# Diagonal blocks of a Gram matrix as high times half of high plus high times low, with their transposes taken up in the head weights

## The reference

```python
mn = (m - mu) * jax.lax.rsqrt(var + EPS) * gamma + beta
q = (mn @ Wq).reshape(N, L, H, C)
k = (mn @ Wk).reshape(N, L, H, C)
...
att = jnp.einsum('slhc,tlhc->sth', q, k) * scale
att = jax.nn.softmax(att, axis=1)
o = jnp.einsum('sth,tlhc->slhc', att, v) * g
```

## Time and profile before

| | us |
|---|---|
| median of 3 runs | 2096.09 |
| lowest and highest | 2093.72, 2096.11 |
| profiled execution, its own time | 2093.88 |
| its span, first to last instruction | 2092.2 |
| PE busy | 1981.6 (95%) |
| DVE busy | 1237.8 (59%) |
| ACT busy | 674.5 (32%) |
| POOL busy | 440.5 (21%) |

### The profile page before, as it was taken

One profiled execution on the slowest core, in us unless ns is written; L12 is line 12 of the kernel. 1 busy time (PEld: TensorE's weight loads), 2 busy tenths in 40 slices (PEclk: granted clock), 3 DMA queues, 4 the chain that ended last, 5 costly groups with the idle time before them and its releaser, 6 DMA issues.

```text
span 2092.2 us, 27450 instructions
## 1 busy us (share of the span) xinstructions
PE 1981.6 (95%) x9540; PEld 1640.6 (78%) x9540; DVE 1237.8 (59%) x2227; ACT 674.5 (32%) x1091; POOL 440.5 (21%) x565
## 2 busy tenths in 40 slices
PE   7999999999999999999999999999999999438898
PEld 6888888888888888788888878888888788327797
DVE  4656565665656556756565565656654478756543
ACT  4422222222222226322222222222222266424454
POOL 3302020211202014302020220202012155422342
PEclk9999999999999999999999999999999999769999
DMA  4232433334343333143333424333334479310110
GB/s 141 91 101 83 156 114 121 101 120 156 94 141 111 122 119 122 61 166 116 121 111 121 149 72 161 110 121 111 111 131 171 176 278 310 124 31 21 41 42 31
DMA packets 88114, 250.14 MB, mean 120 GB/s; under 512 B 11968, under 2 KB 32448, under 8 KB 88000
## 3 DMA queue, kind: packets, MB, share of 16 engines
q1 hardware_dynamic: 84928, 240.27, 34.4%
q0 software_dynamic: 3072, 8.44, 1.3%
HBM read 194.05 MB, written 54.62 MB: 119 GB/s over the span
## 4 chain that ended last, share of the span: by engine, by line
PE 90%; DVE 5%; issue 2%; ACT 1%; DMA 1%; POOL 1%; SPq 0%; DVEq 0%; ACTq 0%; POOLq 0%
PE bank L662 34%; PE bank L677 34%; PE bank L809 4%; PE bank L1563 4%; PE bank L1583 3%; PE bank L712 3%; PE bank L1151 2%; PE bank L634 2%; PE bank L647 1%; PE bank L608 1%; PE bank L618 1%; DVE top_passed L1232 1%; DVE top_counts L1235 0%; DVE top_pivots L1229 0%; DMA prelu<-in_tok_prelu_a 0%
## 5 line engine op out<-in xcount | busy, mean ns | idle before, releaser
L677 PE MATMUL bank<-x_hi,kt 128*128 128x512 f32 x2048 | 724.2, 395 | 1.5 <-DVE work L518 1.4
L518 DVE SCALAR_TENSOR_TENSOR work<-bank,d_col,gate 128x512 f32<-128x512 f32 x512 | 383.9, 750 | 553.7 <-PE bank L677 544.4
L397 ACT ACTIVATE p_hi<-work 128x512 fp32r<-128x512 f32 x512 | 324.1, 633 | 1065.7 <-PE bank L662 1020.6
L677 PEld LDWEIGHTS bank<-x_hi,kt 128*128 128x128 f32 x2048 | 384.4, 188 | 90.7 <-DVE work L518 2.7
L662 PE MATMUL bank<-p_hi,v_hi 128*128 128x512 f32 x1024 | 407.0, 397 | 0.3 <-ACT yT L359 0.2
L662 PE MATMUL bank<-p_hi,v_lo 128*128 128x512 f32 x1024 | 404.1, 395 | 0.0
L662 PE MATMUL bank<-p_lo,v_hi 128*128 128x512 f32 x1024 | 403.4, 394 | 0.0
L677 PE MATMUL bank<-x_lo,kt 128*128 128x512 f32 x1024 | 400.9, 392 | 0.0
L506 DVE TENSOR_TENSOR p_lo<-work,p_hi 128x512 fp32r<-128x512 f32 x512 | 367.7, 718 | 29.3 <-ACT p_hi L397 29.2
L567 POOL TENSOR_SCALAR spread<-mv 128x4 f32<-128x4 f32 x16 | 5.0, 310 | 1125.6 <-DVE mv L450 1125.6
L662 PEld LDWEIGHTS bank<-p_hi,v_hi 128*128 128x128 f32 x1024 | 192.2, 188 | 50.6 <-DVE p_lo L506 5.3
(11 more groups left out here) (227 smaller groups left out, 2281.3 us busy)
## 6 DMA issues: line engine op xcount, KB each, us to landing
gate<-in_gateT SPq DMA_DIRECT2D x256, 512.0 KB, 3.6
work<-in_xT SPq DMA_DIRECT2D x32, 512.0 KB, 4.9
scratch_rows<-rows SPq DMA_DIRECT2D x16, 518.0 KB, 3.8
scratch_h<-work SPq DMA_DIRECT2D x16, 512.0 KB, 3.0
scratch_mn<-mn_sb SPq DMA_DIRECT2D x16, 512.0 KB, 6.8
scratch_mT_hi<-mT_hi SPq DMA_DIRECT2D x16, 512.0 KB, 2.7
scratch_mT_lo<-mT_lo SPq DMA_DIRECT2D x16, 512.0 KB, 4.0
gate<-scratch_mn SPq DMA_DIRECT2D x16, 512.0 KB, 4.4
```

What stands on the lines that cost most here:

```text
L397: nc.scalar.activation(p_hi[:, i % 2, :], p32[:, i % RP, :], ACT.Copy).then_inc(hi_done, 1)
L518: nc.vector.scalar_tensor_tensor(p32[:, i % RP, :], S[i % 2][:, :], d_col[:, i:i + 1], gate[:, g % RG, j, :], ALU.add, ALU.mult).then_inc( ...
L677: mm = pe.matmul(S[i % 2][:, :], w, x, start=n == 1, stop=n == 3 * KD)
```

## The change

The diagonal blocks G(0,0) and G(1,1) are symmetric. With H the high part and L the low part, the block is H^T H + H^T L + L^T H. The changed kernel sums B = H^T (H/2) + H^T L alone, so that B + B^T is the block. It leaves the product low by high out for the diagonal blocks, and in `head_weights` B enters twice: once with Wk first and Wq as the factor, once with Wq first and Wk as the factor. G(0,1) is summed as before.

ACT therefore makes four tiles for each chunk in the place of one instruction: the high parts of entry 0 (`g_own`) and entry 1 (`g_other`), then half of the high part of entry 0 (`g_other`) and of entry 1 (`g_own`), so that `g_other[:, h, :, tile]` is H(0)/2 beside H(1), one moving operand of 512 columns. DVE makes the low part in two instructions, one for each entry. SP's load and PE's first product wait for all four copies.

```diff
@@ -226,8 +226,8 @@
         g32 = gate[:, :, :, :].rearrange("p (h b) g t -> p h b (g t)", h=2)
-        g_hi, g_lo = (W["kt"][:, :, :, :].rearrange("p i k t -> p (i k t)")[:, i * 4 * TPC * D:(i + 1) * 4 * TPC * D]
-                      .rearrange("p (h b n) -> p h b n", h=2, b=2) for i in range(2))
+        g_other, g_own, g_lo = (W["kt"][:, :, :, :].rearrange("p i k t -> p (i k t)")[:, i * 4 * TPC * D:(i + 1) * 4 * TPC * D]
+                      .rearrange("p (h b n) -> p h b n", h=2, b=2) for i in range(3))
         S, Y, TR = pr.banks[0:2], pr.banks[2:4], pr.banks[4:8]
@@ -338,6 +338,7 @@
                 past(sp, g_lo_ok, c - 1)
+                past(sp, g_hi_ok, c * 4 - 4)
                 for s in range(2):
@@ -410,7 +411,8 @@
                 past(act, g_done, c - 1)
-                nc.scalar.activation(g_hi[:, h], g32[:, h], ACT.Copy).then_inc(g_hi_ok, 1)
+                for tile, s, half in ((g_own, 0, 1.0), (g_other, 1, 1.0), (g_other, 0, 0.5), (g_own, 1, 0.5)):
+                    nc.scalar.activation(tile[:, h, s], g32[:, h, s], ACT.Copy, scale=half).then_inc(g_hi_ok, 1)
                 if early(c, 1):
@@ -539,8 +541,10 @@
             def gram(c, h):
-                dve.wait_ge(g_hi_ok, c + 1)
-                nc.vector.tensor_tensor(g_lo[:, h], g32[:, h], g_hi[:, h].bitcast(F32), ALU.subtract).then_inc(g_lo_ok, 1)
+                for s, tile in enumerate((g_own, g_other)):
+                    dve.wait_ge(g_hi_ok, c * 4 + s + 1)
+                    low = nc.vector.tensor_tensor(g_lo[:, h, s], g32[:, h, s], tile[:, h, s].bitcast(F32), ALU.subtract)
+                low.then_inc(g_lo_ok, 1)
                 if early(c, 1):
@@ -698,19 +702,22 @@
                 pe.wait_ge(g_lo_ok, c + 1)
+                pe.wait_ge(g_hi_ok, c * 4 + 4)
                 for j in range(TPC):
-                    for i in range(4):
-                        s, m = i // 2, i % 2
-                        if early(c, 1) and j == 0 and i == 2:
+                    tile = slice(j * D, (j + 1) * D)
+                    for m in range(KD):
+                        cols = slice(j * D + m * P, j * D + (m + 1) * P)
+                        first = early(c, 1) and j == 0
+                        high, low = g_own[:, h, 0, cols], g_lo[:, h, 0, cols]
+                        pe.matmul(G[m][:, 0:2 * D], high, g_other[:, h, :, tile], start=first, stop=False, skip_group_check=True)
+                        pe.matmul(G[m][:, 0:2 * D], high, g_lo[:, h, :, tile], start=False, stop=False, skip_group_check=True)
+                        pe.matmul(G[m][:, D:2 * D], low, g_other[:, h, 1, tile], start=False, stop=False, skip_group_check=True)
+                    for m in range(KD):
+                        if early(c, 1) and j == 0 and m == 0:
                             pe.wait_ge(y_evac, END * 2)
-                        cols = slice(j * D + m * P, j * D + (m + 1) * P)
-                        tile = slice(j * D, (j + 1) * D)
-                        out = G[i][:, 0:2 * D] if s == 0 else G[i][:, 0:D]
-                        for n, (w, x) in enumerate(split_products(
-                                g_hi[:, h, s, cols], g_lo[:, h, s, cols],
-                                g_hi[:, h, s:2, tile], g_lo[:, h, s:2, tile])):
-                            mm = pe.matmul(out, w, x, start=early(c, 1) and j == 0 and n == 0,
-                                           stop=False, skip_group_check=True)
+                        high = g_other[:, h, 1, j * D + m * P:j * D + (m + 1) * P]
+                        pe.matmul(G[2 + m][:, 0:D], high, g_own[:, h, 1, tile], start=first, stop=False, skip_group_check=True)
+                        mm = pe.matmul(G[2 + m][:, 0:D], high, g_lo[:, h, 1, tile], start=False, stop=False, skip_group_check=True)
                     if early(c, 1) and j == 0:
@@ -827,22 +834,23 @@
-        for i, (g0, c0, w) in enumerate(((0, 0, wk), (0, D, wq), (0, D, wk), (2, 0, wk))):
-            if i == 3:
-                pe.wait_ge(prod_ok, 1)
+        for i, (g0, c0, w) in enumerate(((0, 0, wk), (0, 0, wq), (0, D, wq), (0, D, wk), (2, 0, wk), (2, 0, wq))):
+            if i >= 3:
+                pe.wait_ge(prod_ok, i - 2)
             for m in range(KD):
                 for k in range(KD):
                     mm = pe.matmul(TP[i % 3][:, m, :], grams[:, g0 + k, c0 + m * P:c0 + (m + 1) * P], w[:, k, :],
                                    start=m == 0 and k == 0, stop=k == KD - 1, skip_group_check=True)
             mm.then_inc(tp, 1)
         pe.wait_ge(made, 2 + P // head)
-        for i in range(4):
+        for i, of in enumerate((0, 0, 1, 2, 3, 3)):
             pe.wait_ge(prod_ok, i + 1)
             for j in range(KD):
                 for m in range(KD):
-                    at = 4 * i + 2 * j
+                    at = 4 * of + 2 * j
                     mm = pe.matmul(colp[:, at:at + 2], prod[:, i, m, j * P:(j + 1) * P], heads_in["ones"][:, :],
-                                   start=i == 0 and j == 0 and m == 0, stop=m == KD - 1, skip_group_check=True)
+                                   start=i == 0 and j == 0 and m == 0, stop=m == KD - 1 and i not in (0, 4),
+                                   skip_group_check=True)
         mm.then_inc(col_ok, 1)
@@ -854,7 +862,7 @@
         dve.wait_ge(ld, 16 * 7)
-        for i, w in enumerate((wq, wk, wq, wq)):
+        for i, w in enumerate((wq, wk, wk, wq, wq, wk)):
             dve.wait_ge(tp, i + 1)
@@ -947,7 +955,7 @@
-            sp.wait_ge(pr.sem("hw_tp"), 4)
+            sp.wait_ge(pr.sem("hw_tp"), 6)
             sp.dma_start(mlp_raw["w1"], ins["ffn_w1"].rearrange("(k p) n -> p k n", p=P)).then_inc(raw_ld, 16)
@@ -1662,7 +1670,7 @@
                     [(x, [P, KD, width]) for x in ("v", "g", "k", "q", "o_wr")] + [("o", [P, KD, width + 2])] +
-                    [("prod", [P, 4, KD, width]), ("same_head", [P, P]), ("ones", [P, 2]), ("cols", [P, 16]),
+                    [("prod", [P, 6, KD, width]), ("same_head", [P, P]), ("ones", [P, 2]), ("cols", [P, 16]),
                      ("att", [P, 2, 2, 2]), ("top", [P, 2, 2]), ("shifted", [P, 2, 2, 2]), ("expd", [P, 2, 2, 2]),
                      ("total", [P, 2, 2]), ("inv", [P, 2, 2])])}
                 start_mix(pr, W2, heads_in, M, scratch, pr.last_mnT)
```

## The result

Seven executions of each kernel give a median of 2095.17 us before and 2088.77 us after. The ratio is 0.9968, with a 95% interval from 0.9956 to 0.9979: 6.7 us faster (4.4 to 9.2). The forecast was 2087.5 us, with 8.6 us to be gained. The direction and the order of size are right; about 2 us of the gain are missing, and they can be found.

What follows compares the result with a forecast made beforehand. PE, busy for 95% of the span, was taken as the bound. Terms of -13.06, -0.74 and +5.20 us summed to -8.6 us: 2085.3 us from the profiled 2093.88, forecast as 2087.5 given the runs' median; range 2083.8 to 2091.8 us.

Steps and rivals of the forecast that it cites:

- Term 1: Gram stage, chunks 1 to 7: fewer long products on PE, 6.58 us a chunk against 8.445, -13.06 us.
- term 2: Gram stage, chunk 0: DVE's chain decides when PE begins chunk 1, 1584.7 us instead of 1585.44, -0.74 us.
- Term 3: Head weights: groups and sums over rows go from 32 to 48 instructions each on PE, +5.20 us.
- The clock rival: After the head weights: low clock may start within the longer sums, -1.8 to +3.6 us; chance 0.12 for the upper half.
- The other rivals: DVE held by POOL (0.08), weights late (0.05), chunk loads as bound (0.04), no gain where claimed (0.05).
- POOL did hold DVE up: Gram stage, subtractions for chunks 2 and 3: each loses 2.1 us to POOL, 3.1 us in all; chance 0.08.
- the row with 4.41 us: Chunk 3 before the change: DVE's subtraction took 4.41 us where 2.3 is usual, beside four POOL additions.
- The chunk loads: Gram stage: loads become the bound if a landing exceeds 8.5 us; about 2100.3 us at 12.7 us landings, chance 0.04.
- The head weights were not late: Ahead of the head weights' use at L816: weights ready at 1635.4 us, PE waits 3.8 us; chance 0.05.

Runs made afterwards that it cites:

- gram_only: Changed kernel's new Gram stage with the old head weights (four groups, diagonal transposes left out), against the kernel before: ratio 0.9946, 11.3 us faster.
- low_first: Changed kernel with DVE's low parts of chunk 1 ahead of rectifying and moments, chunk 2 ahead of normalisation: ratio to the kernel before 0.9955, 9.4 us faster.
- head_only: Old Gram stage with the new head weights (six groups, diagonal blocks counted twice), against the kernel before: ratio 1.0032, 6.7 us slower.
- gram_only_2: Second execution of the new Gram stage with the old head weights, profiled: stage 60.02 us, with a low stretch.
- before_again: The unchanged kernel profiled once more: stage 72.24 us, no low stretch.
- after_again: The changed kernel run again, against the kernel before: ratio 0.9962, 8.0 us faster; stage 60.01 us.
- all_three: Changed kernel with low parts moved up, diagonal groups added by DVE before the sums, and keep_y ahead of ACT's fourth copy: ratio to the kernel before 0.9945.
- low_first_2: Second profiled execution of the changed kernel with DVE's low parts of chunks 1 and 2 moved up: stage 56.18 us, no low stretch.
- after: First profile of the changed kernel: stage 60.02 us with a low stretch; the kernel's median 2088.77 us.
- before: First profile of the unchanged kernel: stage 72.24 us, no low stretch; the kernel's median 2095.17 us.

## Why the prediction was right, and what it lacked

**Term 1 (chunks 1 to 7) and term 2 (chunk 0)** came to 13.8 us in the sum and to 13.77 us in gram_only with the clock up. PE started 0.25 us earlier after the last product of the tokenizer (forecast 0.4) and chunk 1 0.67 us earlier (forecast 0.74). PE's wait ahead of chunk 1 was forecast as 2.2 us and measured as 2.0 us, and its releaser was DVE's low part. Moving that part up (low_first) gave those 2 us back, which shows that the chain through rectifying and moments decided there.

**Term 3 (head weights)**: forecast 5.20 us. The work itself was priced rightly: 3.45 us for the groups and 1.79 us for the sums at the full clock. But to the end of the 48 products it cost 6.2 to 6.3 us in all three profiles, because more work of PE lay in the low stretch, in the sums or behind them. The prediction had put this clock change at nothing; it is the second size that was off, by 1.0 us.

**The step that was mis-sized most** is the price of PE's wait ahead of chunk 1. The prediction took it as 2.2 us, with the clock at the full level behind it. It costs its own length and, in most profiles, another 1.5 us. This is the term by which the stage's gain was 12.2 us instead of 13.8. With the 6.2 us of the head weights the sum is -13.8 + 1.5 + 6.2 = -6.1 us. From the tokenizer's last product to the end of the 48 products, the three profiles of the changed kernel take 100.0 us and the two of before 106.0 us: 6.0 us less. The measured 6.7 us agree with that within their interval. The interval of the ratio would also hold -8.6 us; the stages don't.

**The clock rival** was right in its mechanism and its bounds, but at only one of two places: I looked for a fall in the sums and for a longer low stretch behind them (found, 1.0 us in the changed kernel and 2.7 us in head_only) and not behind the new wait. The Trainium skill (TensorE: Matmul & The Clock Gate, "What's actually happening") says that the monitor runs freely and does not start with the kernel. The trace agrees as far as gram_only and gram_only_2 can show it, with 58.47 and 60.02 us for one and the same kernel, wait and stage. That this is the reason for the difference is not shown.

**The other rivals** did not occur. POOL did hold DVE up: the two subtractions for chunk 3 took together 3.18 us in place of 2.35,

```profile
1588.70 2.35 DVE L546 TENSOR_TENSOR kt<-gate,kt 128x1024 fp32r<-128x1024 f32 x2
1596.14 3.18 DVE L546 TENSOR_TENSOR kt<-gate,kt 128x1024 fp32r<-128x1024 f32 x2 [5.09 <-ACT kt L415]
```

but the loss was 0.8 us, not 4.2, and PE waited for nothing there. That is near to one POOL operation of 0.7 us and so nearer to the lock rule of the Trainium skill (SBUF — State Buffer, "SBUF: two separate sides") than to the row with 4.41 us. Nor does that row stand for the kernel before. In before_again POOL began its four additions as far ahead of DVE, and this time POOL lost the time (4.89 us instead of 2.84) and DVE none:

```profile
1596.27 4.89 POOL L580 TENSOR_TENSOR work<-work,attn_bo 128x256 f32<-128x256 f32 x4
1596.84 2.33 DVE L543 TENSOR_TENSOR kt<-gate,kt 128x2048 fp32r<-128x2048 f32 x1 [6.03 <-ACT kt L413]
```

Which of the two gives way differed between two executions of one kernel; why is not known. The price of this rival was also counted too high: if chunk 2 comes 2.3 us late, PE needs chunk 3 only at 1600.2 us, and even with both losses it is there by then, so the sum is 2.3 us and not 3.1. The chunk loads never held ACT back: it idled for PE alone ahead of its copies of chunks 2 to 7. The head weights were not late; PE had no wait ahead of L816 at 1635.01 us.

**Left open**: what decides in a given execution whether the clock falls behind a wait of 2.0 us, and the rest of the kernel. From the end of the 48 products to the end of the span, ten of the fourteen profiles take 412.9 to 413.4 us. The others take 410.3 (after_again), 410.6 (gram_only_2), 414.2 (low_first) and 416.0 us (all_three), and it is not known why. low_first_2 has 413.4, so the same kernel differs there by 0.8 us, and after_again and after by 2.8 us. A single execution can't show a gain of 6 us to better than that.

## What to carry to other kernels

Where PE is the bound, a sum over its products by the pace of long chains came within 0.1 us here, and a short stall within 0.2 us, by following the one engine that comes late. But a stall of PE had two prices, its length and, in six of eight profiles, 1.5 us for the low clock behind it. So the cheapest gain behind such a change may be to reorder the engine that is late, here 3.8 us for moving DVE's low parts of two chunks up. Many tiny products (two columns each) were a place for a low clock as well, and adding their inputs first on an engine with room took 1.7 to 2.6 us off. And where a low stretch stands, measure to the end of the work that it can reach: a part that ran at the full clock may only have pushed the loss into the next.

## What the runs showed of the hardware that was not expected

- A PE wait of 2.0 us ahead of chunk 1 was followed by a stretch at 1.2 GHz in four of six profiles, one of 2.7 us in two of two; one of 0.55 us or less, or none, in none of six. Each such stretch cost 1.5 us of PE's time. The wait at the start of the stage, 1.0 to 1.75 us, was not followed by one in any of the fourteen; whether it has a share in what happens some 10 us later was not tried.
- The clock can fall while PE shows 6.00 of 6.00 us busy: in the sums with two columns each, 48 instructions took 7.81 us instead of 5.27, with a granted clock of 0.91 from 1662 to 1663 us and 0.50 behind that to their end (head_only).
- DVE's subtraction from SBUF and POOL's additions held each other up in either direction in the same kernel: DVE 4.41 us instead of 2.3 with POOL at its usual 2.84 (before), POOL 4.89 us with DVE at 2.33 (before_again). In the changed kernel both lost: DVE 0.8 us and POOL 2.0 us (4.84 instead of 2.84).
